# Issuing the attention score products of a fused transformer block in pairs of steps

## The reference

```python
x = x + _layernorm(_L0_attn_ref(_layernorm(x), ...))     # 16 heads of 16, causal mask
x = x + _layernorm(_L0_ffn_ref(_layernorm(x), ...))      # 8 experts, the best 2 of each row
...
q = shape_heads((hidden_states @ wq.T + bq) * scaling)
scores = jnp.einsum('bhtd,bhsd->bhts', q, k)
attn = jax.nn.softmax(scores.astype(jnp.float32) + mask, axis=-1).astype(jnp.float16)
out = jnp.einsum('bhts,bhsd->bhtd', attn, v)
```

## Time and profile before

| what | before |
|---|---|
| time, median of 3 runs | 976.39 us (975.93 to 980.9) |
| time of the profiled execution | 978.82 us |
| span of the profiled execution, first to last instruction | 977.1 us |
| TensorE, share of the span busy | 79% |
| VectorE, ScalarE, GpSimd | 66%, 57%, 48% |
| mean granted TensorE clock | 0.759 of 2.4 GHz |

### The profile page before, as it was taken

How to read it: one execution, slowest core, us unless ns; L and a number is a source line. 1 busy time by engine, 2 the same in 40 slices (tenths; PEclk the granted TensorE clock), 3 DMA queues, 4 the chain that set the end, 5 groups by cost and what they waited for, 6 DMA issues and landing times. The chain is left out here.

```text
span 977.1 us, 22077 instructions
## 1 busy us (share of the span) xinstructions
PE 776.4 (79%) x6606; PEld 450.1 (46%) x6607; DVE 649.4 (66%) x2389; ACT 557.2 (57%) x1072; POOL 466.1 (48%) x526
## 2 busy tenths in 40 slices
PE   3488777799989989989989989800999999999700
PEld 1122222233333455545545555500878778778500
DVE  4666768878788778887897876423455555555435
ACT  3588876766646656756756765500454554555326
POOL 3566654672443535765664576453223232332315
PEclk9555555555555589979989998855999999999955
DMA  5343223209110011221112122112433232323264
GB/s 164 119 130 120 90 83 111 70 26 332 60 37 11 25 33 18 52 48 23 27 28 42 19 45 44 15 40 85 109 42 43 38 49 32 49 40 41 28 199 151
DMA packets 69234, 66.39 MB, mean 68 GB/s; under 512 B 5536, under 2 KB 62752, under 8 KB 69152
## 3 DMA queue, kind: packets, MB, share of 16 engines
q1 hardware_dynamic: 55872, 50.86, 17.0%
q0 software_dynamic: 13280, 14.49, 10.6%
HBM read 34.04 MB, written 31.29 MB: 67 GB/s over the span
## 5 line engine op out<-in xcount | busy, mean ns | idle before, releaser
L892 DVE CUSTOM_DVE_ANT_0 unused<-bank,mask 128x384 f16<-128x384 f32 (+3 forms) x512 | 235.3, 484 | 78.2 <-PE bank L1198 74.5
L785 ACT ACTIVATE pT<-bank 128x512 f16<-128x512 f32 (+1 forms) x384 | 201.0, 531 | 121.4 <-PE bank L1207 118.3
L1207 PE MATMUL bank<-qT,kT 32*128 32x384 f16 (+3 forms) x512 | 177.8, 393 | 26.9 <-ACT pT L785 26.1
L1198 PE MATMUL bank<-kT,qT 32*128 32x384 f16 (+3 forms) x512 | 179.1, 399 | 8.2 <-DVE nmax L892 7.7
L1560 POOL DMA_INDIRECT expert_rows<-y_sb,dest x50 | 77.7, 1554 | 174.6 <-DVE y_sb L1683 146.4
L610 POOL TENSOR_SCALAR_AFFINE_SELECT pT<-pT 128x512 f16<-128x512 f16 x128 | 84.5, 704 | 135.0 <-ACT pT L785 134.1
L1723 PE MATMUL bank<-xT,gu_part 128*128 128x256 f16 (+1 forms) x1100 | 131.3, 277 | 3.5 <-issue 2.5
L1723 PEld LDWEIGHTS bank<-xT,gu_part 128*128 (+1 forms) x1100 | 108.0, 101 | 25.4 <-issue 5.5
L1748 PE MATMUL bank<-wd_part,h 128*128 (+2 forms) x850 | 104.5, 273 | 0.6
L1300 PE MATMUL bank<-tile_xT,gu_part 128*128 128x256 f16 (+1 forms) x616 | 92.7, 293 | 9.3 <-DVE stage L1076 9.0
L1207 PEld LDWEIGHTS bank<-qT,kT 32*128 32x128 f16 x512 | 39.6, 97 | 117.1 <-issue 61.7
(11 more groups left out here) (185 smaller groups left out, 1266.4 us busy)
## 6 DMA issues: line engine op xcount, KB each, us to landing
expert_rows<-tile_in SPq DMA_DIRECT2D x1, 8192.0 KB, 26.7
stage<-wg SPq DMA_DIRECT2D x8, 688.0 KB, 4.2
stage<-wu SPq DMA_DIRECT2D x8, 688.0 KB, 4.2
stage<-wd SPq DMA_DIRECT2D x8, 640.0 KB, 4.4
ys<-expert_rows SPq DMA_DIRECT2D x16, 256.0 KB, 5.8
out<-res SPq DMA_DIRECT2D x16, 256.0 KB, 2.1
xin<-dispatch_rows SPq DMA_DIRECT2D x25, 130.0 KB
x_sb<-x SPq DMA_DIRECT2D x8, 256.0 KB
```

The lines of the kernel that those rows point to most:

```text
L785: sc.activation(pT[:, lo:hi], ST_BANK[i % 2][:, 0:hi - lo], ACT.Exp, scale=1.0 / INV_SCALE).then_inc(p_ready, 1)
L892: last = v.tensor_tensor_reduce(out=unused[:, i % 2, at:at + n], in0=S_BANK[i % 2][:, at:at + n], in1=mask[:, T - n:T], scale=-1.0, scalar ...
L1198: last = mm(S_BANK[i % 2][:, at:at + n], qT[32 * j:32 * j + 32, g, P * qt:P * (qt + 1)], kT[32 * j:32 * j + 32, g, 0:n], start=True, stop= ...
L1207: last = mm(ST_BANK[i % 2][:, at:at + n], kT[32 * j:32 * j + 32, g, P * kt:P * (kt + 1)], qT[32 * j:32 * j + 32, g, P * kt:T], start=True, ...
```

## The change

Steps are taken in pairs (i, i+1) with i even.

- TensorE waits at the head of a pair for both exponentials and both maxima of the pair before. Then it issues the four score products of the pair one behind the other: transposed and plain of step i, transposed and plain of step i+1. They use four different row quarters. Behind them, ahead of all other work of the pair, comes `tile_up` of the pair, which was the last but one in the even step. The remaining work of the two steps follows as before, without score products in the middle.
- ScalarE runs both exponentials of a pair first, then the other work of step i (with the tanh), then that of step i+1.
- VectorE runs both maxima first, then `gate` and `product`, then the other work of the two steps.

The number of instructions of each kind, their shapes, the banks and the lists of fills stay as they are. SyncE and POOL are not edited.

```diff
@@ scalar
-                        for i, (j, tiles) in enumerate(FILLS):
-                            lo, hi = P_COL[tiles[0], j], P_COL[tiles[0], j] + width(tiles)
-                            act.wait_ge(st_mm, NF * grp + i + 1)
-                            act.wait_ge(pv_mm, NF * grp + i + 1)
-                            sc.activation(pT[:, lo:hi], ST_BANK[i % 2][:, 0:hi - lo], ACT.Exp,
-                                          scale=1.0 / INV_SCALE).then_inc(p_ready, 1)
-                            n = grp - FIRST_TILE
+                        n = grp - FIRST_TILE
+                        for i in range(NF):
+                            if i % 2 == 0:
+                                for k in (i, i + 1):
+                                    j, tiles = FILLS[k]
+                                    lo, hi = P_COL[tiles[0], j], P_COL[tiles[0], j] + width(tiles)
+                                    act.wait_ge(st_mm, NF * grp + k + 1)
+                                    act.wait_ge(pv_mm, NF * grp + k + 1)
+                                    sc.activation(pT[:, lo:hi], ST_BANK[k % 2][:, 0:hi - lo], ACT.Exp,
+                                                  scale=1.0 / INV_SCALE).then_inc(p_ready, 1)
@@ vector
-                            if n >= 0 and i % 2:
-                                gate(n, i // 2)
-                                product(n, i // 2)
-                            if ahead:
-                                maxima(grp + 2, (g + 2) % G, i)
+                            if i % 2 == 0:
+                                if ahead:
+                                    maxima(grp + 2, (g + 2) % G, i)
+                                    maxima(grp + 2, (g + 2) % G, i + 1)
+                                if n >= 0:
+                                    gate(n, i // 2)
+                                    product(n, i // 2)
@@ tensor
-                            pe.wait_ge(p_ready, NF * grp + i + 1)
-                            scores_kq(g, i)
-                            if ahead:
-                                pe.wait_ge(s_max, NF * (grp + 2) + i - 1)
-                                scores_qk((g + 2) % G, i)
+                            if i % 2 == 0:
+                                pe.wait_ge(p_ready, NF * grp + i + 2)
+                                if ahead:
+                                    pe.wait_ge(s_max, NF * (grp + 2) + i)
+                                for k in (i, i + 1):
+                                    scores_kq(g, k)
+                                    if ahead:
+                                        scores_qk((g + 2) % G, k)
+                                if n >= 0:
+                                    tile_up(n, AT_UP[i], expert[0] * (KD * GU))
@@ tensor, further down in the same step
-                            if n >= 0 and i in AT_UP:
-                                tile_up(n, AT_UP[i], expert[0] * (KD * GU))
```

## The result

The changed kernel takes 1009.32 us (median of 4 runs, 1005.53 to 1010.66); the kernel before, run beside it on the same chip, 977.5 us (975.93 to 980.9). The ratio is 1.0323, 95% interval 1.0287 to 1.036: 3.2% slower, where 1.3% faster was forecast. The profiled execution took 1010.66 us.

A forecast was written before the change was run, and what follows sets the result against it. TensorE was taken as the bound in groups 9 to 17, level with ScalarE before, and busiest, ahead of VectorE, from 18. Terms +3 - 5 - 10 = -12 us took 978.8 to 966.8, 964 us for the median; range 944 to 988.

The forecast's parts named there:

- The gift to TensorE: Score products, groups 0 to 31: a pair takes one slot (0.63 or 0.45 us) instead of two, 106 us less work.
- the 105 named: Sign in groups 9 to 17: TensorE's busy time falls from 127 to below 105 us, showing the bound has moved.
- The held-up quarters: Rival: row quarters start in order, delaying the second step's products in steps 0 to 7; 966 to 972 us, chance 0.07.
- Groups 0 to 8, +3: First attention groups: +0.3 us for each of nine groups, +3 us in all, bounds -4 and +10.
- Groups 9 to 17, -5: TensorE's bound falls and VectorE takes over; four groups gain 1.5 us each, five lose 0.2; bounds -14 and +5.
- the price of a hand-over: From last maximum to next first maximum: product latency plus some 0.1 us for two semaphores, 0.5 to 0.7 us.
- lock-step rival: Rival: each pair takes the longer of ScalarE and VectorE, 0.15 us more in 192 pairs, +29; 981 to 1000 us, chance 0.20.
- Groups 18 to 31, -10: Groups with expert tiles: half of TensorE's relief beyond VectorE's work is lost, leaving 0.7 us gain per group; bounds -35 and +7.
- `gate` and `product` lie behind the maxima and cover VectorE's hand-over: Groups 18 to 31: these two instructions, 0.42 us each, fill VectorE's time during the hand-over.
- The other reason given: Groups 18 to 31: `tile_up` ahead of `values` and projections makes all wait if `product` is late; part of the half lost.
- The granted clock: Sign in 336 to 628 us: prediction fails if it drops well below 0.90; each 10 us at 0.50 adds 5 us work.
- the evacuation binds: Rival: banks are emptied no faster, so hand-overs eat the gains and nothing changes; 972 to 981 us, chance 0.18.

The follow-up runs named there:

- e4: Changed kernel, but TensorE's score products of each step wait only for that step's own two banks; 995.1 us, ratio 1.0205.
- e1: Changed kernel, but in even steps VectorE copies v right behind the two maxima, ahead of `gate` and `product`; 989.48 us, ratio 1.0138.
- e2: Changed kernel, but `gate` and `product` are back at the head of the odd step, maxima still in pairs; 970.93 us, ratio 0.9946.
- e6: Kernel before, nothing in pairs, with only `gate` and `product` moved right behind the even step's maxima; 1032.14 us, ratio 1.0571.
- e3: Changed kernel, but `tile_up` is back at the end of the even step; 1018.51 us, ratio 1.045.
- e5: Changed kernel with the edits of e2 and e4 together; 965.46 us, ratio 0.9865.
- e7: e5 with `tile_up` also back at the end of the even step; 963.64 us, ratio 0.9864.
- e8: Kernel before with TensorE's part alone: paired score products, split waits, early `tile_up`; ScalarE and VectorE as before; 967.58 us, ratio 0.9899.
- e9: e2 from group 18 on; in groups 0 to 17 split waits, with activations and maxima step by step as in e8; 953.32 us, ratio 0.9763.
- e10: e2 with split waits in groups 0 to 17 only, joint waits from group 18 on; 960.53 us, ratio 0.9834.

## Why the prediction was wrong, point by point

**The gift to TensorE: right.** Four starts within 0.02 us, and 0.55 us for a pair at half clock where a step had 0.54, the 0.09 us ahead of the scores left out of both. 106 us of work were to go, and 98 us of busy time went. In groups 9 to 17 TensorE's busy time is 84.6 us, below the 105 named. The held-up quarters did not happen: in group 24 the four long products of steps 4 and 5 start at 491.77 to 491.78, ahead of the short ones at 491.94. (The Trainium skill's rule of strict order, which the prediction quotes, stands on the page that it names in the section "The mechanism".)

**Groups 0 to 8, +3: right, partly by luck.** Measured +0.3 (152.5 to 152.8), group 3 at 14.5. But this was a balance: e4 shows 4.8 us of joint waits in it, and single groups moved by -1.0 (group 5) to +1.6 (group 7).

**Groups 9 to 17, -5: wrong in sign, by 10 us.** Measured +5.3, just beyond the bound of +5; group 15 at 14.1 where 13.5 was taken, group 12 at 16.3 where the sum had 15.5. The four groups 10, 12, 14 and 16, which were to gain 1.5 us each, moved by +1.5, -0.7, +0.6 and -0.6, and the other five lost 4.3 us together where 1.0 was taken. The failing term is the price of a hand-over, "0.5 to 0.7 us" (and 0.65 in group 12): VectorE waited 26.3 us in 25 waits, 1.05 us each. It is the price and not the number: 25 waits in nine groups are about three in each, the least that was taken. In group 12, where the sum had 13.2 us of work and 1.95 of hand-overs, VectorE works 12.1 us and stands idle for 4.2. (From the terms given, group 15 comes to 11.9 to 14.6 and not 12.2 to 14.3.) Before, VectorE waited as well, in shorter pieces:

```profile
DVE unused L892 <- PE bank L1198: 22.0, 36, 1.4
```

The waits are of two kinds. Here are TensorE and then VectorE of the changed kernel in group 15:

```profile
298.37 0.81 PE L1263 MATMUL bank<-ws_part,attT 128*128 128x8 bf16 x24 [1.44 <-ACT attT L701]
```

```profile
299.79 0.56 DVE L895 CUSTOM_DVE_ANT_0 unused<-bank,mask 128x384 f16<-128x384 f32 x1 [1.85 <-PE bank L1203]
...
308.32 0.69 DVE L895 CUSTOM_DVE_ANT_0 unused<-bank,mask 128x512 f16<-128x512 f32 x1 [0.80 <-PE bank L1203]
```

The second wait is a bare hand-over: the last maximum ends at 307.53, the scores start at 307.67, and the next maximum at 308.32. It is 0.80 us, like nine of the 25 (0.79 to 0.81), a little above the 0.7 taken; 0.14 of it lie ahead of the product, where some 0.1 was put down for both semaphores. The first is a hand-over with something in front of it. TensorE stood 1.44 us before the logits, which wait for ScalarE's copy `attT`, and the scores, which start at 299.10, stand behind them in its queue. That copy now comes behind both exponentials; at the same place before, the wait was 0.31 us (292.97). The prediction priced the hand-over by the product's latency and left out what TensorE may be waiting for when the banks come free. e4 prices the joint wait alone: 9.9 us in nine groups, so -4.6 with split waits (130.0 against 134.6), the size that I had forecast. This is the lock-step rival's mechanism, at 17.8 us in all three stages and not 29.

**Groups 18 to 31, -10: wrong, by 35 us, and the cause of the result.** Measured +24.8. The step that failed is "`gate` and `product` lie behind the maxima and cover VectorE's hand-over". It looks at what the two instructions run beside and not at what stands behind them in the queue. There stand the copies that free the one shared bank, and `gate` holds them for as long as it waits for the tanh. I had asked this question of TensorE ("if `product` is late, all of them wait") and not of VectorE, and the rows that point at it, TensorE waiting for v, were in the trace of before with 6.4 us in this stage. e1 puts 21.5 us on the copy of v alone, e2 37.0 on all the even step's work; with `gate` in the odd step this stage takes 280.3 us, 12.2 below before, where -10 was predicted. e6 shows that it doesn't take the pairs, though there the larger part is the wait for the tanh. The other reason given, that `tile_up` ahead of `values` would be paid for, was wrong in sign in the changed kernel (e3), and with `gate` in the odd step its place made no difference (e5, e7).

I also took group 23 as the type of its stage. It is an odd group, and the odd groups hardly moved (136.5 to 135.7). One even group beside it would have shown the copy.

**The granted clock: a sign read rightly, its share open.** "It fails if the clock in 336 to 628 us falls well below 0.90": it fell to 0.86, and the time at half clock rose from 58 to 89 us. Group 24 was at 1.00 before and at 0.69 after. The half-clock time falls again in e1 and e2 (53, 45) and rises in e3 and e6 (98, 131), always with the waits. So in this stage the lower clock goes with TensorE's pauses, and which of the two makes the other isn't shown. (In groups 9 to 17 TensorE's busy time fell from 127 to 85 us, and the granted clock rose from 0.50 to 0.55.) How much of the 24.8 us the clock adds of its own was not isolated; by the prediction's own arithmetic, 31 us more at half clock are at most 15 us of work. e8 shows that a high clock alone doesn't make the stage short: it has the least time at half clock, 30 us, and its groups 18 to 31 still take 294.3 us.

**The rivals.** Lock step was the right side and the smaller half of the cause. That the evacuation binds fits groups 0 to 17: TensorE's work fell by a third there and the groups got no shorter. But order and release of the banks decided, since e9, with the same copies and reductions, takes 16.2 us less for them than the kernel before. The cause of most of the loss was in none of the rivals.

**What stays open.** Why split waits cost time in groups 18 to 31 once `gate` lies in the odd step was not resolved. By the profiled executions it is 8 us (e5 against e2 or e10). By the medians, e5 is 4.9 us above e10, which differs from it in nothing else, but the two were measured on different chips, and the intervals of their ratios overlap; so even the cost is not certain. VectorE's wait for scores is 3.6 us longer in e5 than in e2 (19.6 and 16.0), which is a part of it at most. And moving the copy of v to a bank of its own wasn't tried, since none is free in that stage.

## What to carry to other kernels

When an instruction that waits is moved forward in a queue, list everything that was ahead of it and now is behind, and look up who waits for each: a copy that frees a shared bank can be worth more than the instruction moved. Look at neighbouring periods of the loop, not at one typical one, since rare work is where such waits are. Issue products together, and try letting each wait only for its own bank: it gave 14.7 us in groups 0 to 17 here and nothing sure in the others. Where stages of one loop have different bounds, give each stage its own order, since their gains here added up.

## What the hardware showed

Products of 32 rows on four row quarters started within 0.02 us of one another at both clock levels. From the first start to the next product of 128 rows, a pair with 512 columns took 0.55 us at half clock (501.58 to 502.13) and 0.33 at full clock (505.79 to 506.12), where a step with two quarters had taken 0.54 (302.44 to 302.98) and 0.32 (461.99 to 462.31). So four quarters cost 0.01 us more than two. The Trainium skill's page "TensorE: Matmul & The Clock Gate", section "Measured speedup vs the span model", gives 3.07 times for four row tiles; by it I had worked out an estimated 0.13 us more for a pair at half clock, and the trace doesn't show it. The rest of the surprise was in the program, not in the chip.
